# A four-layer graph network in one launch: where two selector tables, two value buffers and one set of transposes stand in the program

## The reference, cut to what matters

```python
# layer 0: only relation 1 occurs in the drawn adjacency (0 or 1)
h = x @ W_loop.T;  g = h @ Wg_loop.T
vals = (h + b_loop) * sigmoid(g + bg_loop)
out = relu(swap(adj == 1) @ vals)
# layer 1: softmax attention with a bilinear logit, leaky_relu, then elu
# layer 2: 8-head attention, masked by adj, softmax over the 128 neighbours
# layer 3: 8-head graph attention
e = e1[:, :, :, None] + e2[:, :, None, :]      # per head, from h @ W and a
attn = softmax(leaky_relu(where(mask, -inf, e)))
x = attn @ Wh
```

## Time and profile before

| | us |
|---|---|
| median of 3 executions | 719.89 |
| lowest and highest of them | 719.14, 721.03 |
| profiled execution, its own time | 722.2 |
| its span, first to last instruction | 720.3 |
| PE busy | 655.6 (91%) |
| DVE busy | 601.5 (84%) |
| ACT busy | 539.1 (75%) |
| POOL busy | 513.5 (71%) |

### The profile page before, as it was taken

The page is one execution under the profiler, slowest core; times in us unless marked ns, Lnnn a source line. Parts: engine busy times, 40 slices in busy tenths (PEclk is TensorE's granted clock), DMA queues, the critical chain, the costliest instruction groups (busy, mean ns, idle before and its releaser), DMA issues.

```text
span 720.3 us, 17434 instructions
## 1 busy us (share of the span) xinstructions
PE 655.6 (91%) x6378; PEld 491.7 (68%) x6378; DVE 601.5 (84%) x1515; ACT 539.1 (75%) x852; POOL 513.5 (71%) x541
## 2 busy tenths in 40 slices
PE   3999799999699999999999999789999999999972
PEld 2888577777456766666666667567777777777752
DVE  5799669999677988888988986698888888888882
ACT  1555389988478777778777776678899899899882
POOL 6477539899776577776777775467767777767685
PEclk9999899999689999999999999999999999999996
DMA  9900000000000000000000000000000000010001
GB/s 255 278 3 1 2 0 1 2 1 2 0 1 2 2 2 1 2 2 1 2 1 3 2 1 2 1 1 3 18 30 16 15 17 16 19 28 17 16 16 45
DMA packets 28897, 14.91 MB, mean 21 GB/s; under 512 B 1926, under 2 KB 28812, under 8 KB 28812
## 3 DMA queue, kind: packets, MB, share of 16 engines
q1 hardware_dynamic: 25344, 12.59, 6.8%
q10 hardware_dynamic: 3468, 1.20, 0.8%
HBM read 9.59 MB, written 4.19 MB: 19 GB/s over the span
## 4 chain that ended last, share of the span: by engine, by line
PE 48%; DVE 25%; POOL 15%; issue 4%; ACT 4%; DVEq 3%; DMA 1%; ACTq 1%; POOLq 0%
PE pair L1084 15%; POOL arena L667 8%; PE pair L1270 5%; DVE nmx L1000 5%; PE quad L1219 4%; DVE bn L558 3%; DVE arena L994 3%; DVEq L561 3%; POOL yb L674 3%; PE quad L1137 2%; PE pair L1235 2%; POOL ln L526 2%; PE pair L1249 2%; POOL X L533 2%; PE pair L1241 2%
## 5 line engine op out<-in xcount | busy, mean ns | idle before, releaser
L667 POOL TENSOR_TENSOR arena<-arena,nmx 128x1024 f32<-128x1024 f32 x64 | 121.6, 1900 | 74.3 <-DVE nmx L1000 74.3
L645 POOL TENSOR_TENSOR arena<-arena,nmx 128x1024 f32<-128x1024 f32 x64 | 121.4, 1897 | 69.0 <-DVE nmx L1022 69.0
L1084 PE MATMUL pair<-identf,arena 128*128 128x128 f32 x1088 | 151.5, 281 | 0.9 <-DVE yb L1046 0.9
L1084 PEld LDWEIGHTS pair<-identf,arena 128*128 128x128 f32 x1088 | 117.7, 142 | 31.9 <-issue 30.9
L533 POOL TENSOR_SCALAR X<-yb,ln 128x128 f32<-128x128 f32 x256 | 114.7, 461 | 5.1
L526 POOL TENSOR_TENSOR ln<-ln,neghalf 128x4 f32<-128x4 f32 x64 | 66.8, 1044 | 33.6 <-DVE ln L567 33.5
L793 ACT ACTIVATE arena<-quad 128x1024 f32<-128x1024 f32 x64 | 66.2, 1034 | 25.4 <-PE quad L1173 25.3
L1013 DVE TENSOR_TENSOR arena<-quad,mask 128x1024 f32<-128x1024 f32 x64 | 77.7, 1214 | 3.9 <-PE quad L1219 3.2
L1022 DVE TENSOR_REDUCE nmx<-arena 128x8 f32<-128x1024 f32 x64 | 78.0, 1218 | 1.8
L1000 DVE TENSOR_REDUCE nmx<-arena 128x8 f32<-128x1024 f32 x64 | 78.0, 1218 | 1.7
L994 DVE TENSOR_TENSOR arena<-quad,arena 128x1024 f32<-128x1024 f32 x64 | 77.6, 1213 | 2.0 <-ACT arena L793 1.8
(11 more groups left out here) (190 smaller groups left out, 1437.0 us busy)
## 6 DMA issues: line engine op xcount, KB each, us to landing
X<-in_x SPq DMA_DIRECT2D x16, 256.0 KB, 5.5
arena<-in_adj SPq DMA_DIRECT2D x16, 256.0 KB, 5.8
out<-X SPq DMA_DIRECT2D x16, 256.0 KB, 2.3
nat_all<-in_L_gnn_W ACTq DMA_DIRECT2D x2, 64.0 KB, 4.9
w<-in_L_gnn_W ACTq DMA_DIRECT2D x2, 64.0 KB, 5.5
nat_all<-in_L_gnn_W_loop ACTq DMA_DIRECT2D x1, 64.0 KB, 2.7
nat_all<-in_L_gnn_Wg_loop ACTq DMA_DIRECT2D x1, 64.0 KB, 3.3
nat_all<-in_L_gnn_a ACTq DMA_DIRECT2D x1, 64.0 KB, 4.6
```

The costliest lines, as they stand in the source:

```text
L645: nc.gpsimd.tensor_tensor(v3(P2[t % 3], HEADS), v3(P2[t % 3], HEADS), nmx2[t % 2][:].unsqueeze(2).broadcast_to([128, HEADS, N]), ALU.add)\
L667: nc.gpsimd.tensor_tensor(v3(p, HEADS), v3(p, HEADS), nmx2[(t - 1) % 2][:].unsqueeze(2).broadcast_to([128, HEADS, N]), ALU.add)\
L1084: last = nc.tensor.transpose(dst[:, cols(i)], src[:, cols(i)], identf[:])
```

## The change

There are three edits. (1) POOL no longer makes `sel1` and `sel2` in the set-up. The two memsets and six selects stand in layer 2, one in each of the steps 3, 4, 5, 7, 8, 9, 11 and 12, ahead of that step's addition on line 645; PE waits for POOL's counter `pool_set` at 16 before layer 3's first scores. (2) DVE clears `vx` and sets its ones right after it has cleared `bias3`, ahead of the wait for the bias rows and the split. (3) In layer 0 PE's step b goes T(b+1), P(b), Z(b-1) and no longer P(b), T(b+1), Z(b-1).

```diff
+SELECTOR_STEPS = (3, 4, 5, 7, 8, 9, 11, 12)
+POOL_SET = 16
 # POOL, set-up
-            nc.gpsimd.memset(headmask[:], 1.0)
-            nc.gpsimd.memset(sel1[:], 0.0)
-            nc.gpsimd.memset(sel2[:], 0.0).then_inc(sem("pool_set"), 1)
+            nc.gpsimd.memset(headmask[:], 1.0).then_inc(sem("pool_set"), 1)
...
-            for part in range(3):
-                select(sel2[:].rearrange("p (h c) -> p h c", h=HEADS), [[-1, HEADS], [0, 128]], -32 * part)
-                select(sel1[:].rearrange("p (h c) -> p h c", h=HEADS), [[-1, HEADS], [0, 128]], -32 * part - HEADS)
 # POOL, layer 2
+            def selectors(k):
+                nonlocal steps
+                if k == 0:
+                    nc.gpsimd.memset(sel1[:], 0.0).then_inc(sem("pool_set"), 1)
+                    steps += 1
+                elif k == 1:
+                    nc.gpsimd.memset(sel2[:], 0.0).then_inc(sem("pool_set"), 1)
+                    steps += 1
+                    pool.wait_ge(sem("pool_set"), steps)
+                elif k % 2:
+                    select(v3(sel2[:], HEADS), [[-1, HEADS], [0, 128]], -32 * (k // 2 - 1))
+                else:
+                    select(v3(sel1[:], HEADS), [[-1, HEADS], [0, 128]], -32 * (k // 2 - 1) - HEADS)
             def layer2(t):
+                if t in SELECTOR_STEPS:
+                    selectors(SELECTOR_STEPS.index(t))
                 if graph(t):
                     pool.wait_ge(sem("L2_max"), t + 1)
 # DVE, set-up
             nc.vector.memset(bias3[:], 0.0).then_inc(sem("dve_set"), 1)
+            for s in range(2):
+                nc.vector.memset(vx[s][:], 0.0).then_inc(sem("dve_set"), 1)
+            dve.wait_ge(sem("dve_set"), 3)
+            for s in range(2):
+                nc.vector.memset(vx[s][:].rearrange("p (a c) -> p a c", c=HP)[:, :, HD:HD + 1], 1.0)
             dve.wait_ge(sem("dve_set"), 1)
             dve.wait_ge(sem("bias_loaded"), 96)
...
-            for s in range(2):
-                nc.vector.memset(vx[s][:], 0.0).then_inc(sem("dve_set"), 1)
-            dve.wait_ge(sem("dve_set"), 3)
-            for s in range(2):
-                nc.vector.memset(vx[s][:].rearrange("p (a c) -> p a c", c=HP)[:, :, HD:HD + 1], 1.0)
 # PE, layer 0 (the same lines, moved from behind the products to the front)
+                if real(b + 1):
+                    pe.wait_ge(sem(f"x_loaded{b + 1}"), 16)
+                    need(pe, sem("L0_xT"), b + 1)
+                    transposes(bank[0], x_of(b + 1), G).then_inc(sem("L0_xT_mm"), 1)
                 if real(b):
                     pe.wait_ge(sem("L0_xT"), b + 1)
...
-                if real(b + 1):
-                    pe.wait_ge(sem(f"x_loaded{b + 1}"), 16)
-                    need(pe, sem("L0_xT"), b + 1)
-                    transposes(bank[0], x_of(b + 1), G).then_inc(sem("L0_xT_mm"), 1)
 # PE, layer 3
+                if t == 0:
+                    pe.wait_ge(sem("pool_set"), POOL_SET)
```

## The result

The changed kernel takes **716.98 us** (median of 11 runs, 714.14 to 718.42); the kernel before took 721.21 in the runs beside it (11 runs, 718.72 to 722.78). The ratio is 0.9941, interval 0.9926 to 0.9955: faster, by 4.2 us. Forecast were 715.9, that is 4.0 less than the 719.89 of three executions, and a range of 713.8 to 718.2. The profiled execution took 716.22 us, its span 714.4 (before 722.2 and 720.3; forecast 718.2 and 716.3).

The account below looks back on a forecast made before the run. DVE bounds layer 0 from vals(1) on, and its bias split, slowed by POOL's selects, delays the start. Split 3.63 plus transposes 0.43 gives 4.06 us, less 0.1 for layer 2: 719.89 - 4.0 = 715.9 us, range 713.8 to 718.2.

Parts of the forecast that it names:

- The split: DVE set-up: without POOL's selects beside it, the bias split ends at 10.26, not 13.89; 3.63 us less.
- The rival in which the split stays long: DVE set-up: casts are slow for another reason, such as loads beside them; 719.5 us, chance 0.04.
- T(1) ahead: PE, layer 0: T(1) runs in the idle time before P(0), gate(0) follows P(0) at once; 0.43 us less.
- takes what it took, 3.87: PE, layer 0: P(0) starts at about 10.4 and lasts 3.87 us as before, to 14.3.
- the reverse: PE, layer 0: all of P(0) runs at the slow clock, costing 0.3 us; no chance of its own given.
- ACT late next: Layer 0: ACT's six load issues, not PE, delay gate(1), 4.01 us from the first issue; vals(1) at 19.0.
- Same pace after vals(1): DVE, layer 0: 3.61 us per batch stays after vals(1), with vals(15) at 69.5.
- The value buffers: DVE set-up: their clearing is hidden in either place; worth 0, up to 0.3 us.
- The turns in layer 2: POOL, layer 2: the eight memsets and selects mostly fit its idle time; cost 0.1 us, bounds 0 and 8.7.
- The rival at 724.5: Layer 2, steps 3 to 12: all eight memsets and selects delay exponentials and transposes; slower, 724.5 us, chance 0.05.
- Clock sooner (714.2): PE, layer 0: the array's clock rises sooner, making P(0) 1.7 us shorter; 714.2 us, chance 0.15.
- Half the gain goes: Something unseen takes 2 us: late x(1), late bias loads or a longer low clock between layers; 717.9 us, chance 0.14.

Follow-up runs that it names:

- selectors back: Changed kernel with both selector tables made in POOL's set-up again, the other two edits kept: 719.51 us, ratio to the kernel before 0.9976.
- selectors behind split: Changed kernel with the selector tables made in the set-up, but only after the bias split, none in layer 2: 717.79 us, ratio to before 0.994.
- memsets beside split: Changed kernel with ten extra POOL memsets of `sel1` running beside the bias split: 717.36 us (1 run).
- no transposes: Changed kernel with PE's old order in layer 0 (P(b), T(b+1), Z(b-1)): 718.54 us, ratio to the kernel before 0.9965.

## Why the prediction was right

The time was right, and so was the mechanism; that the gain in the medians (4.23 us) came as near to the forecast (4.0) as it did is partly luck. The marks of layer 0 show 3.7, and the profiled execution, forecast at 718.2, took 716.2, because the seams of the layers gave 2.2 us that no term of the sum has.

- **The split.** Forecast 3.63 us shorter, measured 3.70 (6.36 to 2.66). The reason, waiting for POOL's instruction and not for the loads beside it, is shown from several sides: selectors back restores it to the same end although its loads landed later, selectors behind split is as good as the change, and memsets beside split brings it back with other POOL work. The rival in which the split stays long is out.
- **T(1) ahead.** Forecast 0.43. From P(0)'s end to vals(1) are 4.79 us (14.60 to 19.39) against 5.18 before (17.91 to 23.09), 0.39 less; against the changed kernel with the old order it is 0.6 to 0.7 by the traces, and 1.7 by the ratios, which isn't explained. Once the whole start had moved forward, a T(1) left behind P(0) ran partly at the lower clock (0.84 us in no transposes, 0.60 before), so more was to be had by moving it.
- **The mis-sized term: "takes what it took, 3.87".** P(0) started 3.81 sooner but took 0.5 us longer, because more of it lay ahead of the clock's rise. 3.63 + 0.43 = 4.06 had been forecast for vals(1) and vals(15); 3.70 and 3.66 came (3.81 - 0.50 + 0.39 = 3.70 at vals(1)). The text had this as "the reverse" of a rival, at 0.3. Over the profiled executions the term varies by 1.2 us, so it was no number to be had to a tenth.
- **ACT late next.** Right: gate(1) came 4.05 behind the first issue (4.01 taken), PE had ended before it, and putting the issues off moved vals(1).
- **Same pace after vals(1).** Right: 50.53 us from vals(1) to vals(15), before 50.49.
- **The value buffers.** 0 forecast, 0 found.
- **The turns in layer 2.** 0.1 forecast. None shows: the additions of steps 3 and 7 are late by 0.89 and 0.40 us, as forecast, the lead is back in step 8, and the fall left at step 5 is no larger than without turns; the only wait of ACT for POOL lies ahead of the turns. The rival at 724.5 had its point of decision at half of the turns' length. Measured by doubling, some 1.4 of the added 8.5 came through, and that only with the pauses full.
- **Clock sooner (714.2).** Not in the profiled execution, where P(0) was slower than before; in others of the same start it came inside P(0). The changed kernel's fastest run took 714.14, but it has no trace, and the clock at the seams may have done as much for it as P(0).
- **Half the gain goes.** It did not. Of the 4.23 us in the medians the trace explains 3.7; the other half microsecond is less than the marks move between layer 0 and the end from one execution to the next.

## What to carry to other kernels

If DVE's casts and copies end each time just behind an instruction on GpSimd, look for GpSimd work that can lie where DVE waits anyway; here the same work then cost nothing that could be measured, and a pause that is longer than the instruction is the proof to look for. An issue of a DMA held ACT's queue for 0.45 us here, so a batch of six on the engine that makes the first results was worth putting off or spreading. A gain at the start is carried to the end only if the engine that sets the pace never waits in between; check that at two marks inside one layer, and don't price an edit by marks behind a stretch whose clock differs from one execution to the next.

## What the hardware showed that had not been expected

- A DVE cast or copy that begins while a POOL instruction runs ends 0.14 to 0.15 us behind it, whatever its own length: ten of ten, beside memsets of 0.95 to 0.98 us and selects of 1.09 to 1.29. POOL memsets without any input stretch a copy of one row from 0.28 to 1.00 us and casts from 0.29 to between 0.42 and 0.68; a `loopm` (int32 to f32) goes from 0.43 to 1.26 beside a table's memsets.
- The time at which PE's clock reaches its upper level after the start differs between executions of the same instructions by over a microsecond (P(0) took 3.04 us in one and 4.21 in another), and that 12 transposes in the pauses bring it forward isn't shown.
- The first cast, released by the bias loads, starts at 6.9 to 8.0 us with nothing changed in front of the loads.
- In the changed kernel one hundredth more mean granted clock (0.971 to 0.981) goes with 3 to 4 us in the total, with a single run at the upper value.
